# Operand buffers of a two-layer conditioned transformer moved to other distances modulo 512 bytes

## The reference

```python
# first layer: one head of 256 channels
h = film(rmsnorm(x, norm1_w), cond, film1_w, film1_b)
Q, K, V = h @ q_w + q_b, h @ k_w + k_b, h @ v_w + v_b
attn = softmax(einsum('bnd,bmd->bnm', Q, K) * D ** -0.5)
x = x + (einsum('bnm,bmd->bnd', attn, V) @ proj_w + proj_b)
h = film(rmsnorm(x, norm2_w), cond, film2_w, film2_b)
x = x + gelu(h @ mlp_w1 + mlp_b1) @ mlp_w2 + mlp_b2          # hidden width 1024
# second layer: 16 heads of 16 channels, gates from the condition
shift_a, scale_a, gate_a, shift_m, scale_m, gate_m = split(silu(c) @ w_ada + b_ada, 6)
k, q, v = split(modulate(ln(x), shift_a, scale_a) @ w_qkv, 3)   # per head
y = softmax(q / 16 @ k.T) @ v
x = x + gate_a * (y @ w_proj + b_proj)
h = gelu(modulate(ln(x), shift_m, scale_m) @ w_mlp1 + b_mlp1)
x = x + gate_m * (h @ w_mlp2 + b_mlp2)
```

## Time and profile before

| | us |
|---|---|
| median of three timed runs | 1627.81 |
| lowest, highest | 1626.68, 1630.12 |
| span of the profiled execution, first to last instruction | 1626.9 |

### The profile page before, as it was taken

How to read it: one execution, slowest core, us unless ns; L and a number is a source line. 1 busy time by engine, 2 the same in 40 slices (tenths; PEclk the granted TensorE clock), 3 DMA queues, 4 the chain that set the end, 5 groups by cost and what they waited for, 6 DMA issues and landing times.

```text
span 1626.9 us, 42734 instructions
## 1 busy us (share of the span) xinstructions
PE 1600.1 (98%) x14558; PEld 1441.2 (89%) x14558; DVE 1263.6 (78%) x2892; ACT 848.1 (52%) x1696; POOL 484.6 (30%) x639
## 2 busy tenths in 40 slices
PE   8999999999999999999999999999998999999999
PEld 7999999999999998777777777777767999999999
DVE  5798887676666667788888888888885777777776
ACT  3666664333333344666776677767765333333332
POOL 2333331222121123243433344343424222222221
PEclk9999999999999999999999999999999999999999
DMA  6600001000000001332333333332331111111111
GB/s 177 208 20 22 20 16 54 5 1 1 0 0 0 0 2 41 108 111 96 107 103 112 102 103 105 104 109 98 109 116 35 40 44 49 39 52 39 39 52 39
DMA packets 103438, 100.68 MB, mean 62 GB/s; under 512 B 18672, under 2 KB 93872, under 8 KB 103360
## 3 DMA queue, kind: packets, MB, share of 16 engines
q1 hardware_dynamic: 103200, 99.61, 19.5%
q0 software_dynamic: 160, 0.04, 0.1%
HBM read 38.62 MB, written 8.55 MB: 29 GB/s over the span
## 4 chain that ended last, share of the span: by engine, by line
PE 94%; DVE 3%; ACT 1%; DMA 1%; issue 1%; SPq 0%; DVEq 0%; ACTq 0%
PE bank L207 66%; PE bank L1619 7%; PE bank L1601 7%; PE bank L1563 5%; PE bank L329 4%; PE bank L1629 2%; PE bank L1637 1%; PE bank L696 1%; PE bank L400 1%; PE bank L189 1%; PE bank L491 0%; DMA A_w_film<-in_L_cond_film_w 0%; DVE m_xhat L1575 0%; DVE C_negmax L1575 0%; DMA C_qs<-C_q_lo 0%
## 5 line engine op out<-in xcount | busy, mean ns | idle before, releaser
L1710 ACT ACTIVATE C_probs<-bank 128x1024 f32<-128x1024 f32 x256 | 262.6, 1026 | 154.6 <-PE bank L1601 154.3
L1575 DVE TENSOR_REDUCE C_negmax<-bank 128x4 f32<-128x1024 f32 x248 | 303.3, 1223 | 48.7 <-PE bank L1563 45.1
L983 ACT ACTIVATE B_g<-bank,B_bias 128x256 f32<-128x256 f32 x256 | 107.6, 472 | 210.8 <-PE bank L207 210.8
L983 ACT ACTIVATE D_g<-bank,D_bias 128x256 f32<-128x256 f32 x256 | 107.5, 472 | 210.4 <-PE bank L207 210.4
L296 POOL TENSOR_TENSOR m_rstd<-m_var,neghalf 128x2 f32<-128x2 f32 x64 | 52.2, 815 | 509.2 <-DVE m_var L287 259.6
L1601 PEld LDWEIGHTS bank<-C_qs,C_kx 64*128 64x128 f32 x1024 | 77.4, 185 | 79.4 <-ACT C_probs L1710 45.8
L207 PE MATMUL bank<-m_h_hi,B_wt_w_lo 128*128 128x256 f32 x512 | 147.5, 288 | 0.0
L207 PE MATMUL bank<-m_h_hi,D_wt_w_lo 128*128 128x256 f32 x512 | 146.9, 287 | 0.4 <-DVE m_h_lo L348 0.4
L207 PE MATMUL bank<-D_wt_w_hi,D_g_lo 128*128 128x256 f32 x512 | 145.7, 285 | 0.2
L207 PE MATMUL bank<-m_h_lo,B_wt_w_hi 128*128 128x256 f32 x512 | 144.8, 283 | 0.0
L207 PE MATMUL bank<-D_wt_w_lo,D_g_hi 128*128 128x256 f32 x512 | 144.6, 282 | 0.0
(11 more groups left out here) (257 smaller groups left out, 4994.9 us busy)
## 6 DMA issues: line engine op xcount, KB each, us to landing
C_qs<-C_q_hi SPq DMA_DIRECT2D x128, 128.0 KB
C_kx<-C_k_hi SPq DMA_DIRECT2D x128, 128.0 KB, 2.6
C_qs<-C_q_lo SPq DMA_DIRECT2D x64, 128.0 KB
C_kx<-C_k_lo SPq DMA_DIRECT2D x64, 128.0 KB, 2.1
C_gbc<-mod_rows SPq DMA_DIRECT2D x32, 256.0 KB, 3.4
D_gbc<-mod_rows SPq DMA_DIRECT2D x32, 256.0 KB, 3.3
out<-xres SPq DMA_DIRECT2D x31, 256.0 KB, 3.5
xres<-in_x SPq DMA_DIRECT2D x4, 1792.0 KB, 11.0
```

The costliest lines, as they stand in the source:

```text
L983: ins = eng.activation(g[u][:, d * S:(d + 1) * S], hbank[u][:, d * S:(d + 1) * S], func, bias=per_seq(bias1, 2 * u + d, b))
L1575: e_max.by(eng.tensor_reduce(m4[:, :, :, j], spair[:, :].rearrange("p (e q k) -> p e q k", e=2, q=TH), AX, ALU.max, negate=True))
L1710: e_exp.by(eng.activation(probs[t % NP][:, :], stpair[:, :], ACT.Exp, scale=scl))
```

## The change

Only places change. Gaps that nothing reads (`gap_...`) are allocated between operand buffers, the norms' small tiles are joined into one strip for each norm (`small`), the constants `neghalf`, `ones` and `zero` into another (`consts`), and some small buffers (`scale1m`, `shift1m`, the bias columns `bcol`) are allocated elsewhere. The instructions, their shapes, their order and their waits are the same.

From the sizes in the code follow these residues (address modulo 512) and distances (stationary minus moving, modulo 512):

| product | stationary, before to after | moving, before to after | distance, before to after |
|---|---|---|---|
| A q | m: 352 to 224 | a_h: 160 to 64 | 192 to 160 |
| A v | a_h: 160 to 64 | vp: 352 to 192 | 320 to 384 |
| A scores | q: 480 to 128 | a_h: 160 to 64 | 320 to 64 |
| A AV | pT: 96 to 32 | v: 480 to 128 | 128 to 416 |
| B up | w1: 480 to 384 | m_h: 352 to 64 | 128 to 320 |
| B down, u = 0, 1, 2, 3 | g: all 384 to 384, 448, 480, 32 | w2: 448 to 64 | all 448 to 320, 384, 416, 480 |
| C k and q | w: 384 to 384 | a_h: 160 to 64 | 224 to 320 |
| C v | a_h: 160 to 64 | w: 384 to 384 | 288 to 192 |
| C projection | y: 320 to 32 | w: 384 to 384 | 448 to 160 |
| D up | w1: 352 to 384 | m_h: 352 to 64 | 0 to 320 |
| D down, u = 0, 1, 2, 3 | g: all 384 to 416, 448, 480, 32 | w2: 384 to 384 | all 0 to 32, 64, 96, 160 |

In C the buffers of the heads' products (`kx`, `qs`, `probs`, `vaug`) move too, but the distances within their products stay at 0.

```diff
+SMALL = 24
+G_GAPS = ((0, 16, 8, 16), (8, 8, 8, 16))
+Y_GAP = 16
...
-        neghalf = sb("neghalf", [P, TH])
-
+        small = {n: sb(n + "small", [P, SMALL]) for n in ("a_", "m_")}
         scale0m = sb("scale0m", [P, KT * NB])
         scale1a, shift1a = sb("scale1a", [P, KT * NB]), sb("shift1a", [P, KT * NB])
-        scale1m, shift1m = sb("scale1m", [P, KT * NB]), sb("shift1m", [P, KT * NB])
-        one_rows, zero_col, rows = sb("ones", [P, 1]), sb("zero", [P, 1]), sb("rows", [P, 2 * D])
+        rows = sb("rows", [P, 2 * D])
...
-                self.stat = sb(name + "stat", [P, TH * 6])
-                self.mv = sb(name + "mv", [P, TH * 2])
-                self.var = sb(name + "var", [P, TH])
-                self.msq = sb(name + "msq", [P, TH])
-                self.rstd = sb(name + "rstd", [P, TH])
+                t = small[name]
+                self.stat, self.mv = t[:, 0:6 * TH], t[:, 6 * TH:8 * TH]
+                self.var, self.msq, self.rstd = (t[:, TH * c:TH * (c + 1)] for c in (8, 9, 10))
...
         attention_norm, mlp_norm = NormBuffers("a_"), NormBuffers("m_")
+        scale1m, consts = sb("scale1m", [P, KT * NB]), sb("consts", [P, 8])
+        neghalf, one_rows, zero_col = consts[:, 0:TH], consts[:, TH:TH + 1], consts[:, TH + 1:TH + 2]
...
                 biasq = sb("biasq", [P, KT * NB])
+                sb("gap_m", [P, 96])
                 m_hi, m_lo = sb("m_hi", [P, KT * D], F32R), sb("m_lo", [P, KT * D], F32R)
+                sb("gap_vp", [P, 120])
                 vp_hi, vp_lo = sb("vp_hi", [P, KT * D], F32R), sb("vp_lo", [P, KT * D], F32R)
...
+                sb("gap_q", [P, 80])
                 q_hi, q_lo = sb("q_hi", [P, KT * S], F32R), sb("q_lo", [P, KT * S], F32R)
...
+                sb("gap_pT", [P, 72])
                 pT_hi, pT_lo = sb("pT_hi", [P, TH * S], F32R), sb("pT_lo", [P, TH * S], F32R)
...
+                self.bcol = sb("bcol", [P, HT])
+                if not layer:
+                    sb("gap1", [P, 16])
                 self.w = [Weight(sb, sem, "w1", a[n1])]
...
-                g_hi = [sb(f"g_hi{u}", [P, 2 * S], F32R) for u in range(4)]
-                g_lo = [sb(f"g_lo{u}", [P, 2 * S], F32R) for u in range(4)]
+                g_hi, g_lo = [], []
+                for u, gap in enumerate(G_GAPS[l1]):
+                    if gap:
+                        sb(f"gap_g{u}", [P, gap])
+                    g_hi.append(sb(f"g_hi{u}", [P, 2 * S], F32R))
+                    g_lo.append(sb(f"g_lo{u}", [P, 2 * S], F32R))
...
                         qk = {n: sb(n, [P, KT * S], F32R) for n in ("q_hi", "q_lo", "k_hi", "k_lo")}
+                        sb("gap_x", [P, sum(G_GAPS[1])])
...
+                sb("gap_y", [P, Y_GAP])
                 y_f, y_hi, y_lo = sb("y_f", [P, KT * S]), sb("y_hi", [P, KT * S], F32R), sb("y_lo", [P, KT * S], F32R)
...
             mlp0 = Mlp(0, sb_near, sem_near)
+            shift1m = sb_near("shift1m", [P, KT * NB])
+            sb_near("gap2", [P, 16])
             mlp0.w.append(Weight(sb_near, sem_near, "w2", a["L0_cond_mlp_w2"]))
```

More of the change, by code:

```diff
@@ L870, in __init__ @@
                 self.layer = layer
+                self.bcol = sb("bcol", [P, HT])
+                if not layer:
+                    sb("gap1", [P, 16])
                 self.w = [Weight(sb, sem, "w1", a[n1])]
                 self.b1, self.b2 = a[c1], a[c2]
-                self.bias1, self.bcol = sb("bias1", [P, HT * NB]), sb("bcol", [P, HT])
+                self.bias1 = sb("bias1", [P, HT * NB])
                 self.s_b, self.s_mm = sem("b"), sem("mm")
```

## The result

The kernel after takes 1617.52 us (median of 4 runs, 1615.32 to 1619.21) against 1627.49 for the kernel before (median of 4 on the same chip, 1626.68 to 1630.12): a ratio of 0.9933, 95% interval 0.9919 to 0.9948. That is 10.0 us faster; 11.3 were predicted. The profiled execution of after, the slowest of its four, has a span of 1617.4 us and a time of 1619.21, so 1.8 us lie around a span.

A forecast was written before the change was run, and what follows sets the result against it. TensorE, in flight 98% of the span, was taken to bound the kernel. Terms summed to 14.2 us, less 2.15 (D) and 0.78 (C): 11.3 us, span 1615.6, plus 0.9 gives 1616.5 us; range 1602 to 1627.

The forecast's parts named there:

- The distance sets the pace: All mm3 matmuls: stationary minus moving address modulo 512 sets the pace, by up to 5 ns in 119.
- rival 1: Low paces of v and scores belong to their neighbours in A; up stays at 119, no change, 1627.8 us; chance 0.11.
- B, 7.9 us of the sum: Stage B gains: up 128 to 320, 6.45 us; down g0 448 to 320, 0.96; down g1 to g3, 0.48.
- D up, 5.07 us: Stage D up, distance 0 to 320: 3.3 ns x 1536 matmuls gained, 5.07 us.
- C, 0.78 us: Stage C: half of its 1.57 us taken off, since TensorE's waiting for other engines there was unknown.
- New distances, read off a circle of 512 bytes: Unmeasured distances, mostly in A, B down, D down: line through known paces, each value possibly off by 3 ns.
- What would have shown it: Signs: B and D up at 114.5 to 116 ns, longer wait before D down 1, scores slower, v a little.
- the prediction's last line: Prediction wrong if paces do not follow the table or new distances spread wider than 114.5 to 119.2.
- D's chain, 2.15 us off: D's loop: VectorE's order of splits and residual turns 0.098 us a sequence into waiting, 22 sequences, 2.15 us.
- The rule that TensorE's reads wait for nobody: TensorE's operand reads: two read ports of its own, so addresses cost nothing and the change gives 1627.8 us.
- rival 2: Most new distances are good, at 114.5 ns: A gains 4.6 us, about 15 us more overall, 1601; chance 0.09.
- rival 3: Scores and D down g0 to g2: slow hump between distances 0 and 128; at 130 ns, 1634 us; chance 0.07.

The follow-up runs named there:

- all at 64: Kernel after with both MLPs, first attention, C's q, k and projection at distance 64 modulo 256, C v at 192: 1613.77 us, ratio 0.9921 against before.
- the kernel with everything: Kernel after with distances 64 modulo 256, group 1 of B and D down at 384, D laid out like B, GpSimd's additions later: 1600.48 us, ratio 0.9828.

## Why the prediction was right, step by step

The time and the range hold and the mechanism of the forecast holds; several terms of the sum were wrong in ways that cancelled, so that the sum came within 1.3 us of the gain is in part luck.

- *The distance sets the pace.* Right, by the runs up put back and by the shift of 32 bytes; rival 1 (place) falls with them. It is not the whole: at the good distance a run goes at 113.4 or 117.8 ns, depending on what ran before it. The earlier trace rows had shown it: the two runs of scores at 320, 117.3 and 114.5 ns, were put down as one place with a mean of 115.9.
- *B, 7.9 us of the sum.* Measured 9.6 by the steady sequences and 8.5 by the whole stage. Up was put at 115.0 ns, a run of A, and got 113.7: 5.5 ns x 1536 = 8.4 us in place of 6.45. Group 0 gained 4.1 ns in place of 2.5.
- *D up, 5.07 us.* It went from 118.5 to 115.4 by the mean, 3.1 x 1536 = 4.8 us: D's runs up are a mixture of the two paces, three fast or nearly so for one slow, and the slow one is up 0.
- *C, 0.78 us.* Measured nothing: k and q, now at 320, still took 116 to 117 ns, and the projection went from 117.6 to 119.5. For k and q it is the second pace again: in after 13 of 32 runs of k are fast and 17 slow, 8 and 24 of q. With all at 64, where k and q have the same distance as in after and the projection another, 29 of 31 runs of k are fast and 12 of 32 of q.
- *New distances, read off a circle of 512 bytes.* This step failed. 64 was put at 118.75 and measured 114.9 in the scores and 115.5 in D's group 1; 384 was put at 116.25 and measured 118.1 to 118.5; 416 at 116.9 and 119.6 to 119.9; 480 at 118.1 and 116.6. Only 32, 96 and 160 were about right (118.3, 118.6, 118.9 to 119.5). I smoothed over 512 bytes what repeats after 256; the point at 288, which lay off the line, was the sign of it, being 32. What would have shown it is thus half wrong too: the scores did not become slower, and v lost 3.5 ns and not 1.25. B's groups 1 to 3 lost 0.7 us where 0.48 was to be gained, A 1.6 where 1.27 was put down. The spread, 113.3 to 119.9, is a little wider than 114.5 to 119.2, which by the prediction's last line speaks against it.
- *D's chain, 2.15 us off.* That a chain takes a part is right: the unrolled sequences gained 0.165 us, those of the loop 0.105, so 22 x 0.06 = 1.3 us were lost, and the wait before down 1 grew. The link was wrong. I named VectorE's order with the residual in it; it is the rounding of group 1 beside GpSimd's additions, as the later additions show (4.8 us faster, the residual left in its place).
- *From the span to the time.* I added 0.9 us; a run lies 1.8 us above its span, so the profiled execution of before, 1626.9, was a slower one than the median of 1627.81. The forecast of the span was 1615.6 us. The profiled one had 1617.4, but it was the slowest of four; the median less 1.8 is 1615.7. Between the two profiled executions B gave 0.6 us more than put down by the whole stage (8.5 against 7.9) and A, C and the overlap of C with D some 2.4 less.
- *The rule that TensorE's reads wait for nobody* (the Trainium skill, SBUF — State Buffer, "Who interferes with whom") would have given 1627.8. The measurement decides against that here: B up has 113.7 and 118.4 ns in two kernels that differ in addresses alone. What in TensorE waits, if anything does, no run shows.
- *Rivals 2 and 3.* Of the new distances only 64 was good (rival 2; its 4.6 us of A is the difference to the forecast, the gain itself would be 3.3). A hump between 0 and 128 there is not; the low point lies there (rival 3).

## What to carry to other kernels

When equal matmuls follow each other back to back, take their pace from the starts, product by product, and lay it beside the addresses of the next weights and the moving operand; here one distance in eight, 64 modulo 256, was worth 3 to 6 ns in 119 when its fast pace was reached. A good layout may hold only in one of two states, so look at the spread of the runs and not at their mean, and test whether a run of another kind in between restores it. Where an engine in order feeds the next stage, compare the length of the same operation from place to place: one that takes twice its usual time may have company on another engine, and moving that company may cost nothing.

## What the runs showed of the hardware

Paces in ns a matmul (128 x 128 stationary, 128 x 256 moving, at the granted clock 1.00), by the distance modulo 256, from before, after and the shifted kernel:

| modulo 256 | paces, where |
|---|---|
| 0 | 118.5 D up, 119.2 D down (0) |
| 32 | 118.2 C v (288), 118.3 D down g0 (32), 118.2 B up (288) |
| 64 | 113.4 to 113.7 B up and g0 (320), 114.9 scores (64); or 117.8 |
| 96 | 118.6 D down g2 (96), 117.8 to 118.4 B down (352) |
| 128 | 119.2 B up (128), 118.1 B down g1 (384), 118.5 A v (384) |
| 160 | 119.2 A q (160), 118.9 D down g3 (160), 119.6 B down g2 (416) |
| 192 | 117.9 A q and 117.0 C v (192), 117.7 B down (448) |
| 224 | 117.0 C q (224), 116.6 B down g3 (480) |

Pairs that differ by 256 agree within 1.1 ns, but for 64 against 320, where two paces mix. In B, where all runs have the same two addresses modulo 512, a run at 64 modulo 256 keeps the pace, 113.4 or 117.8, that it is handed, through as many as eight runs; in D, where up and down have different ones, it does not. A pause can change it (the four transposes, or in the kernel with everything a wait of 0.05 us ahead of down 0, after which two runs had 117.8), and a run at 384 brought the fast pace back in nearly every sequence seen. In B the start behind the transposes tells something of it: with all at 64, the first interval of up 3 was 206 or 207 ns in 11 sequences, all fast, and 200 to 202 in 20, of which 18 were slow. What happens in the weight load or the stream in either state, and why the sequences of B came as fast, slow, slow, stays open: the records show only that the weight loads of the slow state last 187 to 192 ns and those of the fast state 187 to 188.
